# A four-layer graph network kernel: operands laid out transposed on the host, and a new order of blocks over seven stages

## What is computed

```python
# layer 0: 8 heads of width 32
Xp = X @ Wp + bp;  Xc = Xp @ C^T (per head)
out0 = relu(tanh(A * (Xc @ Xp^T)) @ Xp)
# layer 1: hypergraph convolution twice, H = (adj != 0), w = first row of adj
conv(x, W) = D^-1 H B^-1 H^T (x @ W^T) + b
out1 = conv(layernorm(relu(conv(x, W1))) * gamma + beta, W2) + x
# layer 2: T = rows of A * exp(leaky_relu(sj + si + ab)), normalised
out2 = relu(x @ Wk0 + T (x @ Wk1 + T (x @ Wk2)) + biases)
# layer 3: xg = x * sigmoid(deg * Wd + bd); QK = sigmoid(xg @ Wqk^T + bqk)
out3 = relu((normalised(QK QK^T * A)) @ xg @ Wl^T + bl + xg @ Wr^T)
```

## Time and profile before

| | |
|---|---|
| median of 3 runs | 2132.2 us (2131.32 to 2135.13) |
| span of the profiled execution | 2128.7 us |
| busy: PE, DVE, ACT, POOL | 1964.9, 1660.7, 1271.3, 862.6 us |
| TensorE's mean granted clock | 0.986 |
| DMA, share of 16 engines | 14.0% |

### The profile page before, as it was taken

One profiled execution on the slowest core, in us unless ns is written; L12 is line 12 of the kernel. 1 busy time (PEld: TensorE's weight loads), 2 busy tenths in 40 slices (PEclk: granted clock), 3 DMA queues, 4 the chain that ended last, 5 costly groups with the idle time before them and its releaser, 6 DMA issues.

```text
span 2128.7 us, 52096 instructions
## 1 busy us (share of the span) xinstructions
PE 1964.9 (92%) x15270; PEld 1659.1 (78%) x15270; DVE 1660.7 (78%) x4520; ACT 1271.3 (60%) x2508; POOL 862.6 (41%) x1677
## 2 busy tenths in 40 slices
PE   3799999999999999999999999999999999999995
PEld 3678787887887887888878878878788788788773
DVE  4478788878788888888878888878887878888873
ACT  2356666666665666666666666666666666566653
POOL 0134444434435434434434444444443443543443
PEclk8799999999999999999999999999999999999998
DMA  3011111111111111111111111111111111111100
GB/s 109 28 43 45 42 49 44 42 49 44 42 49 52 35 49 52 37 50 52 38 48 49 44 42 49 44 42 49 44 42 49 44 42 49 52 35 49 52 25 23
DMA packets 106517, 97.20 MB, mean 46 GB/s; under 512 B 12928, under 2 KB 97664, under 8 KB 106496
## 3 DMA queue, kind: packets, MB, share of 16 engines
q1 hardware_dynamic: 106496, 96.94, 14.0%
HBM read 29.79 MB, written 16.78 MB: 22 GB/s over the span
## 4 chain that ended last, share of the span: by engine, by line
PE 45%; DVE 25%; issue 14%; ACT 10%; POOL 5%; DVEq 1%; SPq 0%; ACTq 0%; DMA 0%; POOLq 0%
PE psum L983 27%; DVE stats L669 5%; PE psum L1162 3%; PE psum L996 3%; PE psum L1105 3%; PE psum L1113 3%; ACT z L600 3%; PE psum L1034 2%; DVE res L882 2%; DVE hid L704 2%; DVE hid_stats L802 2%; POOL hid_rstd L422 2%; DVE xT_lo L662 2%; ACT hid_relu L507 2%; ACT e_neg L584 2%
## 5 line engine op out<-in xcount | busy, mean ns | idle before, releaser
L413 POOL TENSOR_TENSOR xg_lo<-xg,xg_hi 128x512 fp32r<-128x512 f32 x64 | 82.5, 1289 | 649.1 <-ACT xg_hi L463 649.1
L481 ACT ACTIVATE x<-res,shift,rstd 128x256 f32<-128x256 f32 x512 | 280.2, 600 | 13.6 <-POOL shift L395 12.2
L463 ACT ACTIVATE xT_hi<-psum 128x512 fp32r<-128x512 f32 x128 | 76.7, 599 | 306.7 <-PE psum L996 306.7
L669 DVE BATCH_NORM_STATS2 stats<-res 128x6 f32<-128x256 f32 x512 | 192.8, 419 | 8.9
L983 PE MATMUL psum<-wk_hi,xT_hi 128*128 128x258 f32 (+1 forms) x512 | 192.8, 377 | 1.1 <-DVE xT_lo L662 1.1
L388 POOL TENSOR_TENSOR var_eps<-mean_var,eps 128x2 f32<-128x2 f32 x256 | 50.6, 198 | 349.9 <-DVE mean_var L678 349.9
L392 POOL TENSOR_TENSOR rstd<-var_eps,minus_half 128x2 f32<-128x2 f32 x256 | 179.3, 700 | 20.0
L600 ACT ACTIVATE z<-hid_relu,hid_bias,hid_rstd 128x512 f32<-128x512 f32 x128 | 97.5, 809 | 137.9 <-POOL hid_bias L425 137.9
L983 PE MATMUL psum<-wk_hi,xT_lo 128*128 128x258 f32 (+1 forms) x512 | 174.2, 340 | 0.0
L983 PE MATMUL psum<-wk_lo,xT_hi 128*128 128x258 f32 (+1 forms) x512 | 173.8, 340 | 0.0
L689 DVE TENSOR_TENSOR masked<-psum,adjT 128x512 f32<-128x512 f32 x256 | 158.4, 682 | 6.9 <-PE psum L1013 6.9
(11 more groups left out here) (190 smaller groups left out, 6397.8 us busy)
## 6 DMA issues: line engine op xcount, KB each, us to landing
x_in<-in_x SPq DMA_DIRECT2D x64, 256.0 KB, 2.8
x<-x_in SPq DMA_DIRECT2D x64, 256.0 KB, 2.3
adjT<-adjT SPq DMA_DIRECT2D x128, 128.0 KB, 2.0
out<-x SPq DMA_DIRECT2D x64, 256.0 KB, 2.2
adj_in<-in_adj SPq DMA_DIRECT2D x64, 128.0 KB, 2.5
adj_spare<-adjT SPq DMA_DIRECT2D x64, 128.0 KB, 1.9
adjT<-adj_spare SPq DMA_DIRECT2D x64, 128.0 KB, 2.0
wk_f<-in_L_gnn_Wk SPq DMA_DIRECT2D x3, 256.0 KB, 6.1
```

The source lines that it names most:

```text
L413: pool.tensor_tensor(xg_lo[:, :, :, :], xg[:, :, :, :], value(xg_hi[:, :, :, :]), ALU.subtract) \
L463: return act.activation(dst, src, ACT.Copy).then_inc(sem(name), 1)
L481: last = act.activation(xs[k + 1][:, g, :], res[k][:, g, :], ACT.Identity, scale=rstd[k][:, g:g + 1], bias=shift[k][:, g:g + 1])
L669: last = dve.bn_stats(stats[k][:, g, :], res[k][:, g, :])
```

## The change

x's transpose, adj's transpose and all transposed weights come from the host: `xt` (pairs, 128, 512) and `adj_t` (pairs, 128, 256) are new inputs, the weights come as four blocks `w0` to `w3` and four rows `v0` to `v3`. The transposes of x and adj on PE, ACT's copy of adj's transpose and the four copies from SBUF to SBUF are gone. Each of the four layers loads its own adj into `adjT[k]` out of DRAM; x is loaded into `xs[0]` out of DRAM.

There are 7 stages and 70 turns (ramp 0 to 5, loop 6 to 63, drain 64 to 69). On PE only stages 0 to 4 have work. The order on PE is now: `hop2`; `zT_0`, `zT_1`; `qkT`; `y1_0`, `y1_1`; `gram`; `conv`; `headsT`; `rz_0`; `heads`; `rz_1`; `xp`; `mix_0`, `xT2`, `prop`, `xpT`, `mix_1`, `deg`; `y0_0`; `pxT`, `xcT`; `y0_1`, `si`; `hid_0`, `hid_1`, `y12_0`, `y12_1`; `xT3`; `hop1_0`, `hop1_1`; `scores0_of(0)`, `scores0_of(1)`. Banks are given out anew. `xT0_lo` goes from DVE to POOL, reading `xt_in`. Two columns of sums are read by one DVE instruction (`both`), `deg_p` is folded into `node_r`, a copy of one column of adj becomes a product with ones, POOL's doubling of x1 falls away (weights and eps are scaled), and POOL's addition to `qk` becomes a `tensor_scalar`.

SP's turn, after (all of it), and what it replaces in before (cut):

```diff
-                if on[0]:
-                    await_on_sp("xT0", p[0])
-                    await_on_sp("x0_copied", p[0], 16)
-                    sp.dma_start(x_in[:, :, :], pair_at(x, x_at)).then_inc(sem("x_loaded"), 16)
...
-                    sp.dma_start(xs[0][:, :, :], x_in[:, :, :]).then_inc(sem("x0_copied"), 16)
...
+                if on[4]:
+                    await_on_sp("scores", p[4])
+                    await_on_sp("deg", p[4])
+                    sp.dma_start(adjT[3]..., rows_at(adj_t, (t.i - 4) * (G * P * P))).then_inc(sem("adj3_loaded"), 16)
+                if on[0]:
+                    await_on_sp("xT0_hi", p[0])
+                    await_on_sp("xT0_lo", p[0])
+                    sp.dma_start(xt_in..., rows_at(xt, t.i * (G * P * D))).then_inc(sem("xt_loaded"), 16)
+                if on[3]:
+                    await_on_sp("alpha", p[3])
+                    sp.dma_start(adjT[2]..., rows_at(adj_t, (t.i - 3) * (G * P * P))).then_inc(sem("adj2_loaded"), 16)
+                if on[1]:
+                    await_on_sp("inc", p[1])
+                    await_on_sp("edge_w", p[1])
+                    sp.dma_start(adjT[1]..., rows_at(adj_t, (t.i - 1) * (G * P * P))).then_inc(sem("adj1_loaded"), 16)
+                if on[6]:
+                    await_on_sp("x4", n[6])
+                    sp.dma_start(pair_at(out, (t.i - 6) * (G * P * D)), xs[4][:, :, :]).then_inc(sem("stored"), 16)
+                if on[2]:
+                    await_on_sp("res0", p[2])
+                    sp.dma_start(xs[0][:, :, :], pair_at(x, (t.i - 2) * (G * P * D))).then_inc(sem("x0_loaded"), 16)
+                if on[0]:
+                    await_on_sp("masked_3", p[0])
+                    sp.dma_start(adjT[0]..., rows_at(adj_t, t.i * (G * P * P))).then_inc(sem("adj0_loaded"), 16)
```

The start of DVE's turn, after (cut):

```diff
+                if on[1]:
+                    mask(3, n[1], p[1])
+                if on[2]:
+                    read_y1(1, n[2], p[2])
...
+                if on[4]:
+                    wait(dve, "mix_1", p[4])
+                    wait(dve, "adj3_loaded", n[4], 16)
+                    wait(dve, "gram", n[4])
+                    dve.scalar_tensor_tensor(out=scores[:, :, :], ...).then_inc(sem("scores"), 1)
+                if on[2]:
...
+                    last.then_inc(sem("res1"), 1)
+                    layer_stats(1, n[2])
+                    aggregate(1, n[2], p[2])
+                if on[3]:
+                    layer_stats(2, n[3])
+                if on[1]:
+                    wait(dve, "x1", p[1])
+                    wait(dve, "x0_loaded", n[1], 16)
+                    wait(dve, "heads", n[1])
+                    dve.tensor_tensor(res[0][:, :, :], ps("heads")..., xs[0][:, :, :], ALU.add).then_inc(sem("res0"), 1)
+                    layer_stats(0, n[1])
+                    aggregate(0, n[1], p[1])
+                if on[3]:
+                    aggregate(2, n[3], p[3])
+                if on[0]:
+                    wait(dve, "headsT", p[0])
+                    wait(dve, "xp", n[0])
+                    dve.tensor_tensor(xp[:, :, :], ps("xp")..., bias(bp_bc, [P, G, D]), ALU.add).then_inc(sem("xp_read"), 1)
```

And on PE:

```diff
-                    wait(pe, "x_loaded", n[0], 16)
-                    turned("xT0", x_in)
-                    wait(pe, "adj_loaded", n[0], 16)
-                    claim("adjT", t)
-                    for g in range(G):
-                        last = pe.transpose(ps("adjT")[:, g * P:(g + 1) * P], adj_in[:, g, :], ident[:, :])
-                    last.then_inc(sem("adjT"), 1)
```

More of the change, by code:

```diff
@@ L36 @@
 LAYERS = 4
-STAGES = LAYERS + 1
-NORM_STAGE = [1, 1, 2, 4]
+STAGES = 7
 LN_EPS = 1e-5
+W0, W1, W2, W3 = NC * D + NC * P, NC * HID + NK * D + 2 * NK, 4 * NC * D, NC * D + 2 * NC * D + 3 * NC
+V0, V1, V2, V3 = D, HID + D, D + 2 * D + 3 * D + 1, D
 BANKS = 8
 TENANTS = [
[L45 to L49, removed]
[5 rows of a table removed]
-    ("y1_1", 3, 1, "y1_read_1"), ("headsT", 7, 0, "headsT_read"), ("gram", 0, 3, "scores"),
-    ("conv", 4, 1, "res1"), ("heads", 7, 0, "res0"),
-]
[L59 to L63, removed]
[4 rows of a table added]
+    ("prop", 5, 1, "prop_read"), ("xpT", 3, 0, "xpT_read"), ("mix_1", 7, 4, "mix_read_1"), ("deg", 4, 3, "gate"),
[5 rows of a table added]
+]
+PARTS = {"y12": 2, "y12_read": 2, "y0": 2, "y0_read": 2, "hid": 2, "hid_read": 2, "hid_relu": 2, "rz": 2,
+         "rz_read": 2, "hop1": 2, "hop1_read": 2, "zT": 2, "zT_hi": 2, "zT_lo": 2, "mix": 2, "mix_read": 2,
+         "tanh": 2, "hid_pow": 2, "deg_inv": 2, "y1": 2, "y1_read": 2, "att": 4, "masked": 4, "edge": 2,
+         "rows": 2, "attn": 2, "pow0": 2, "pow1": 2, "pow2": 2, "pow3": 2}
 def part_of(name):
@@ L268, in wait, with turns, once @@
                 eng.wait_ge(sem(name), value)
-        def turns(eng, turn):
+        def turns(eng, turn, prepare):
+            def once(i):
+                for at, job in prepare:
+                    if at == i:
+                        job()
             for i in range(STAGES - 1):
+                once(i)
                 turn(eng, Turn(eng, i))
@@ L533, in turn @@
-                if on[1]:
-                    wait(act, "prop", n[1])
-                    wait(act, "conv", p[1])
-                    wait(act, "node_r", p[1])
+                if on[3]:
+                    wait(act, "si", p[3])
+                    wait(act, "y12_1", p[3])
+                    wait(act, "y0_1", p[3])
+                    wait(act, "xT2_lo", p[3])
+                    wait(act, "xT2", n[3])
+                    hi(xT2_hi[:, :, :, :].rearrange("p c g n -> p (c g n)"), ps("xT2"), "xT2_hi")
@@ L581, in turn @@
+                if on[4]:
+                    wait(act, "xT3", p[4])
+                    wait(act, "res3", p[4])
+                    normalise(2, n[4])
+                if on[3]:
+                    wait(act, "e_exp", p[3])
+                    wait(act, "sj5", n[3])
+                    wait(act, "si", n[3])
                     for g in range(G):
@@ L651, in _ @@
-            act.wait_ge(sem("consts"), 3)
-            turns(act, turn)
+                if on[4]:
+                    wait(act, "mix_1", p[4])
+                    wait(act, "mix_read_1", p[4])
+                    wait(act, "rz_0", n[4])
+                    act.activation(rz3[:, 0, 0:2 * D], ps("rz_0"), ACT.Copy).then_inc(sem("rz_read_0"), 1)
+                if on[2]:
+                    wait(act, "xT2", p[2])
+                    wait(act, "res2", p[2])
+                    normalise(1, n[2])
@@ new lines, in turn @@
+                if on[4]:
+                    wait(dve, "x4", p[4])
+                    wait(dve, "mix_read_1", n[4])
+                    dve.scalar_tensor_tensor(out=res[3][:, :, :], in0=mix[:, :, :], scalar=0.0, in1=xs[3][:, :, :],
+                                             op0=ALU.max, op1=ALU.add).then_inc(sem("res3"), 1)
+                if on[1]:
+                    wait(dve, "hid_1", p[1])
+                    wait(dve, "pxT_hi", n[1])
+                    lo(pxT_lo[:, :, :, :].rearrange("p c g n -> p (c g n)"), ps("pxT"),
+                       value(pxT_hi[:, :, :, :]).rearrange("p c g n -> p (c g n)"), "pxT_lo")
@@ L829, in turn @@
[L829 to L843 removed]
+                    mask(0, n[0], p[0])
@@ new lines, in turn @@
+                if on[2]:
+                    y1_of(0, t, n[2])
+                    y1_of(1, t, n[2])
+                if on[4]:
+                    wait(pe, "qk", n[4])
+                    claim("gram", t)
+                    for g in range(G):
+                        for c in range(NC):
+                            last = pe.matmul(ps("gram")[:, g * P:(g + 1) * P], qk[:, c, g, :], qk[:, c, g, :],
+                                             start=c == 0, stop=c == NC - 1)
+                    last.then_inc(sem("gram"), 1)
```

1290 lines of the change are left out of this document (613 added, 677 removed), and 14 rows, old and new, of the table TENANTS.

## The result

The changed kernel takes 2181.49 us (median of four runs, 2175.11 to 2183.57), the kernel before 2133.28 on the same chip: a ratio of 1.0228 [1.0208, 1.0248], **2.3% slower**. The prediction was 2113 us, 0.9% faster. The number lies outside its range, 1998 to 2160.

What follows compares the result with a forecast made beforehand. The prediction took PE, 95% busy at full clock, as the bound: 29.13 us of work plus waits of 0.39 and 1.92 make 31.44 a turn; 60 turns, 223.0 outside and 3.5 to the median give 2113 us, range 1998 to 2160.

Steps and rivals of the forecast that it cites:

- the landing of x: Load of x into `xs[0]`: lands 2.8 us after SP issues it, like today's `x_in`.
- SP's queue: x issued sixth behind `scores`, five steps in 3.38 us; DVE's `res0` gets late and PE waits 1.92 us before `xpT`.
- rival C: Slower: the same wait before `xpT` grows; at 0.76 us a step the time equals before, at 0.90 2178 us; chance 0.20.
- the predicted turn: One loop turn: 29.13 us of PE work, 0.39 at `hop2` and 1.92 before `xpT`, 31.44 us.
- PE's floor: PE's work in a loop turn without waits: 30.22 less 0.66 and 0.43, 29.13 us, at most 29.56.
- the span-to-median term: Added to the predicted span: the median of the runs lies 3.5 us above the profiled span.
- PE's work: Loop turn on PE: removing the transposes of x and adj saves 0.66 us, shorter tails and fewer fp32r groups 0.43.
- The tails: PE rows in front of gaps: modelled tails vanish and fp32r products form five groups, not six; 0.43 us a turn.
- PE's old gaps: PE's waits in the loop: `xp` gone, nothing taken for `zT` (0.4 us if its chain grows), `hop2` keeps 0.39 us.
- Outside the loop: Preparation, ramp and drain: 7 us less than 230.0, so 223.0 us, bounds 205 and 240.
- B: x lands in time and PE keeps only the gap at `hop2`: turn 29.52, 1998 us; chance 0.27.
- D: `gram` gets late on POOL, `xT0_lo` standing ahead of `qk` at 1.29 us each: 0.3 us late gives 2131 us; chance 0.11.

Runs made afterwards that it cites:

- x_first: The changed kernel with the load of x put first among SP's seven issues of a turn, ahead of the wait for `scores`: 1967.97 us, 0.9227 of before.
- late_dve: x_first with DVE's addition for `res0` done seven times instead of once, so DVE is late with no transfer late: 2272.3 us.
- with_transposes: x_first with six transposes of the identity a turn put on PE ahead of `xp`: 2008.81 us, 0.9427 of before.
- before_host_t: The kernel before with x and adj transposed on the host, PE's transposes and two copies gone, block order kept: 2132.37 us, 1.0004 of before.

## Why the prediction was wrong, by its own steps

**The step that failed** is the landing of x in the part on SP's queue: "The load has the size and form of today's `x_in`, 2.8 us from issue to landing." A load with other transfers around it is not one by itself. As sixth of a burst it took 3.5 us in the median and 3.68 to `res0`. In x_first the same load, at the head of the burst, lands in 2.8; in fourth, fifth or sixth place in 3.4 to 3.6. The text had this under rival C ("each may land later than alone") but put no number on it. In the turn shown it is 0.88 us, and the chain outgrew its count by 0.86: the other links together were right. Over the loop the wait takes 2.59 us of the turn at full clock (31.77 less x_first's 28.77 and 0.41 at `hop2`), not 1.92: 0.67 us a turn, 40 us in all. While the burst runs, the DMA engines are 71% busy (the row from 1052 us above); that the transfers delay each other there is my reading of it and was not tested by itself.

Both figures that the text took from the Trainium skill (DMA: Bandwidth & Descriptors, Anatomy of one DMA) stand there for a transfer that GpSimd issues, while SP issues x. By its formula the load takes 2.6 us (an estimate), further from the 3.5 here than the row's 2.8. Its 50 ns are a part of one transfer, not the distance of two issues; SP's stood 0.67 to 0.74 us apart.

**What was missing altogether** is the clock, a term that the sum had at nothing, and it is the larger part of the miss. None of the prediction's terms or rivals had PE at anything but full clock, since before showed no fall in its loop. PE's wait brings falls in 34 of 58 turns, 0.97 us a turn, 58 us in all. late_dve shows the falls with a wait and no late transfer, x_first shows neither. Mean waits for `xp` of 0 and 1.2 us a turn brought no falls, 1.75 ten, 2.5 thirty-four, 3.1 fifty-three, in 58 turns each.

In numbers, from the predicted turn: 31.44 - 0.36 (PE's floor lower than said) + 0.02 (`hop2`) + 0.67 (wait, 2.59 instead of 1.92) = 31.77, + 0.97 (clock) = 32.74 us, measured 32.73. 60 x 1.29 = 77 us more, 5 us less outside the loop, and 3.5 us taken off the span-to-median term, which was nil here: 2113 becomes 2181.5.

**What was right.**
- PE's work: 0.66 us for the transposes, 0.65 in with_transposes. The tails were worth more: x_first's turn less its wait is 28.77 us, where the text had 29.13, so 0.79 instead of 0.43.
- PE's old gaps: `xp` and `zT` gone, `hop2` 0.41 where 0.39 was worked out.
- SP's queue: x as sixth behind `scores`; five steps in 3.48 us against 3.38; DVE idle before `res0` for the DMA; PE's longest wait before `xpT` released by the reading of `xp`. PE's work in the chain was 8.02 us (x_first, 1006.87 to 1014.89) against 8.05. That the five steps came out so near is in part luck: the text gave 0.62 us to a step with one wait and 0.14 more to one with a second. The rows show 0.67, 0.67 and 0.74 with one wait, 0.67 and 0.73 with two, so the second wait shows no cost of 0.14 and the plain step takes more than said; the two errors largely cancel. In the earlier trace rows, 0.13 of the 0.28 us between the two steps is the longer issue row (0.50 against 0.37), which the text took for waits.
- Outside the loop: 217.7 against 223.0; the first product starts at 17.5 us, where 19 was estimated.

**The rivals.** B (x in time, 1998 us) was not this kernel but x_first: 1968 us, 30 below (0.34 us of each turn's floor and `hop2` are 20, the ramp 7, the span-to-median term 3); the mechanism was priced about right, and only SP's order stood between the two. C (slower) is the outcome, but not at its price: this went by the steps on SP, and they took 0.70 us each, under the 0.76 that it needed. The wait grew by the landing, which C only names, and the falls of the clock did the rest: with the falls taken out, 60 x 31.77 + 217.7 = 2124 us (an estimate), it would be 9 us faster than before. D fell: POOL's new form for `qk` takes 0.71 us instead of 1.29, and it ended in time:

```profile
...
1011.27 1.29 POOL L357 TENSOR_TENSOR xT_lo<-xt_in,xT_hi 128x512 fp32r<-128x512 f32 x1
1014.00 0.71 POOL L362 TENSOR_SCALAR vec<-vec 128x512 f32<-128x512 f32 x1 [1.44 <-ACT vec L525]
```

(the second row is it; it waits for ACT, not for `xT0_lo`, the first row). Where the text says that the rows of before leave PE as the bound of the turn, before_host_t shows more: taking work from PE alone gave nothing, since a ring of PE and DVE set the turn; PE's way through the same stretch was 0.3 us shorter, the gap before `xp`. The gain of x_first, 164 us, is therefore not the transposes' alone; in the old order they gave nothing. The prediction asked of each removed microsecond what covers it, but not what ring runs parallel to PE at that length; that this did not matter was luck, since the new order had moved `xT0_lo` away from DVE (no run tests this move by itself).

## What to carry to other kernels

Before moving a load in a queue, write down its slack to the instruction that needs it, and price it at its landing in the burst in which it will be, not alone: here 0.7 us at each place and 0.6 to 0.8 of landing. Put first in the queue what is needed first, above all ahead of a wait for a late producer; one load moved was worth 213 us. And a wait of PE that recurs each turn can cost more than itself, so look at the granted clock of the turns behind it; while an engine at 95% busy need not be the bound: take a little work off it, and if the time stays, look for the ring.

## What the runs showed of the hardware

- The granted clock fell to half for stretches of 3.4 us in a loop where PE was busy about 90% of the time (29.92 of 33 us), right behind a wait of 2.5 us in the mean. Each cost 1.6 to 1.7 us. That a single gap a turn would do it, I had not expected. The Trainium skill (TensorE: Matmul & The Clock Gate, Part 1) says that activity releases a throttle and its absence brings it back; the runs agree, with every fall of after at the end of PE's wait. Why it falls in 34 of 58 turns and not in the others was not tested: the waits before either are alike in after (2.54 and 2.46 us in the mean).
- The load of 256 KB landed 0.6 to 0.8 us later in fourth to sixth place of a burst of transfers issued 0.7 us apart on one queue than at its head (3.4 to 3.6 against 2.8 us), with the DMA engines 12% busy over the whole turn and 71% in the burst. `xt_in`, of the same size and second in the burst, still landed in 2.8.
- A two-element copy on DVE took 1.27 us beside POOL's addition, a reduction of the same elements 0.15, and then the next `tensor_scalar` 0.70 instead of 0.17: here the hold-up went on to the next `tensor_scalar`, which ended within 0.03 us of POOL's instruction in all 61 turns in which they met. The two reductions ahead of it did not show it (0.15 and 0.42).
